# A recurrent network's kernel: TensorE's two nested loops become one flat loop whose jump lies between two matmul groups, and GpSimd's sums lose their start gates

## What is computed

```python
Xz = jnp.einsum('btc,hc->tbh', X, Wxz) + bxz          # and Xr, Xh alike
def step(H, xs):
    Z = jax.nn.sigmoid(xz + H @ Whz.T + bhz)
    R = jax.nn.sigmoid(xr + H @ Whr.T + bhr)
    H_tilda = jnp.tanh(xh + R * H @ Whh.T + bhh)
    H_new = Z * H + (1.0 - Z) * H_tilda
    Y = H_new @ Whq.T + bhq
    return (H_new, Y)
_, Ys = jax.lax.scan(step, h0, (Xz, Xr, Xh))
x = x + jnp.transpose(Ys, (1, 0, 2))
```

## Time and profile before

| | |
|---|---|
| median of 3 runs | 2247.37 us (2243.91 to 2275.53) |
| the profiled execution | 2232.23 us, its span 2230.3 us |
| PE busy | 2132.6 us, 96% |
| DVE, ACT, POOL busy | 71%, 55%, 40% |
| TensorE clock granted | 0.998 of full speed (2.4 GHz) |

### The profile page before, as it was taken

How to read it: one execution, slowest core, us unless ns; L and a number is a source line. 1 busy time by engine, 2 the same in 40 slices (tenths; PEclk the granted TensorE clock), 3 DMA queues, 4 the chain that set the end, 5 groups by cost and what they waited for, 6 DMA issues and landing times.

```text
span 2230.3 us, 206497 instructions
## 1 busy us (share of the span) xinstructions
PE 2132.6 (96%) x88464; PEld 2054.4 (92%) x88464; DVE 1589.5 (71%) x9106; ACT 1226.0 (55%) x5994; POOL 888.9 (40%) x1830
## 2 busy tenths in 40 slices
PE   8899999999999999999999999999999999999997
PEld 7799999999999999999999999999999999999997
DVE  4777777777777777777777777777777777777776
ACT  2455555555555555555555555555555555555554
POOL 3344344444344443444443444434444434444331
PEclk9999999999999999999999999999999999999999
DMA  3000000000000100000000000000000000000000
GB/s 153 16 28 17 26 24 21 26 24 21 26 24 19 28 17 26 24 21 26 24 21 26 23 19 28 16 26 24 21 26 24 21 26 24 19 28 16 26 20 22
DMA packets 84278, 58.27 MB, mean 26 GB/s; under 512 B 9490, under 2 KB 75410, under 8 KB 83474
## 3 DMA queue, kind: packets, MB, share of 16 engines
q1 hardware_dynamic: 84240, 57.81, 8.7%
q10 hardware_dynamic: 4, 0.02, 0.0%
HBM read 41.01 MB, written 16.78 MB: 26 GB/s over the span
## 4 chain that ended last, share of the span: by engine, by line
PE 95%; issue 4%; DMA 1%; DVE 1%; ACT 0%; SPq 0%; DVEq 0%
PE u_bank L620 42%; PE v_bank L620 20%; PE y_bank L555 9%; PE d_bank L523 7%; PE b_bank L523 6%; PE a_bank L523 6%; PE c_bank L523 3%; DMA w_all<-in_w_x 0%; PE b_bank L540 0%; PE a_bank L540 0%; PE u_bank L540 0%; DVE pre_t L980 0%; PE c_bank L540 0%; DMA y_io<-in_x_res 0%; DVE scanned L1082 0%
## 5 line engine op out<-in xcount | busy, mean ns | idle before, releaser
L980 DVE STREAM_TRANSPOSE pre_t<-u_bank 128x32 f32<-128x32 f32 (+1 forms) x3072 | 455.1, 199 | 278.2 <-PE u_bank L620 241.4
L620 PE MATMUL u_bank<-wh,scanned 128*16 128x128 f32 (+1 forms) x16384 | 548.5, 273 | 82.8 <-issue 74.9
L317 POOL TENSOR_TENSOR x_parts<-z_of 128x96 f32<-128x96 f32 x744 | 341.6, 459 | 556.7 <-DVE h_sums L1000 243.1
L620 PE MATMUL u_bank<-wh,reset_state 128*16 128x128 f32 (+1 forms) x16384 | 556.4, 273 | 3.7 <-DVE reset_state L1133 2.5
L620 PE MATMUL v_bank<-wh,scanned 128*16 128x128 f32 (+1 forms) x16384 | 548.1, 273 | 0.0
L620 PEld LDWEIGHTS u_bank<-wh,scanned 128*16 128x16 f32 (+1 forms) x16384 | 428.5, 103 | 112.4 <-issue 103.7
L620 PEld LDWEIGHTS v_bank<-wh,scanned 128*16 128x16 f32 (+1 forms) x16384 | 460.9, 104 | 0.3 <-issue 0.2
L620 PEld LDWEIGHTS u_bank<-wh,reset_state 128*16 128x16 f32 (+1 forms) x16384 | 428.4, 103 | 18.2 <-DVE reset_state L1133 14.0
L968 ACT ACTIVATE scan_on<-pre_t 128x16 f32<-128x16 f32 (+1 forms) x1536 | 237.8, 219 | 288.8 <-DVE pre_t L980 288.8
L942 ACT ACTIVATE r_gate<-pre_t 128x16 f32<-128x16 f32 (+1 forms) x1536 | 234.5, 215 | 255.4 <-DVE pre_t L980 247.9
L317 POOL TENSOR_TENSOR z_of<-z_of 128x96 f32<-128x96 f32 x558 | 255.9, 459 | 275.5 <-DVE reset_state L1133 173.1
(11 more groups left out here) (141 smaller groups left out, 2848.9 us busy)
## 6 DMA issues: line engine op xcount, KB each, us to landing
y_io<-in_x_res SPq DMA_DIRECT2D x256, 64.0 KB, 2.0
out<-y_io SPq DMA_DIRECT2D x256, 64.0 KB, 1.6
x_all<-in_x_t SPq DMA_DIRECT2D x62, 256.0 KB, 2.6
w_all<-in_w_x SPq DMA_DIRECT2D x2, 1536.0 KB, 7.6
wh<-in_w_hr SPq DMA_DIRECT2D x1, 1024.0 KB, 10.7
wh<-in_w_hz SPq DMA_DIRECT2D x1, 1024.0 KB, 14.2
wh<-in_w_hh SPq DMA_DIRECT2D x1, 1024.0 KB, 16.2
wq<-in_w_q SPq DMA_DIRECT2D x1, 1024.0 KB, 6.4
```

The lines of the kernel that those rows point to most:

```text
L317: nc.gpsimd.tensor_tensor(*of, ALU.add).then_inc(made, 1)
L620: mm = nc.tensor.matmul(gate_rows(g, par, slice(Q * j, Q * j + rows)), of, wh[g][:, m, P * j:P * (j + 1)], start=False, stop=(m == G - 1), ...
L980: nc.vector.transpose(flat(pre_t[g][:, a:b]), gate_part(g, par, a, b)).then_inc(done, 1)
```

## The change

On PE, `half_turn` becomes `steps`, which starts with Z of its first step and ends with R of the next half's first step; one flat loop ("four_steps") over four steps takes the place of the two nested ones, so the jump back stands between R and Z. The loop's counters are registers, added to between matmul groups, and the hint for the jump's target is given once, in the body's first step. Which of the two products lists runs is chosen by a register, `begins`. The last three halves are written out behind the loop. The waits for `u_put` and `v_put` move: `u_put` to a place ahead of gap work in the step before, `v_put` in front of R's last four matmuls. Waits for `x_loaded` and `s_ready` move from PE to ACT, ahead of the copies that PE waits for anyhow, and waits for weight sums move to the block that needs them. On POOL, all four gates go, and with them the increments of `kept_ready` on DVE.

```diff
                 elif before:
-                    after_sums(2 * n)
                     combine_x2(6, n - 2)
                     combine_x2(7, n - 2)
-                    after_reset(t)
                     combine_21(3, n - 2)
-                    after_kept(t)
                     combine_21(4, n - 2)
-                    after_state(t + 1)
                     combine_21(5, n - 2)
...
-            def half_turn(i, t, x_gap, first=False, end=False):
...
+            def steps(at, x_gap, within=None, end=False, first=False):
...
                 for c in range(4):
-                    par, s = divmod(c, 2)
...
-                    recur(R, t + c, c)
+                    if c > 0:
+                        recur(R, t + c + 1, c, i if c == 2 and not first else None)
+                        if within is not None and c > 1:
+                            within(c)
                     if first and c == 0:
                         plain_to(2, a_bank)
...
-                    recur(Z, t + c, c)
+                    recur(Z, None, c, first=first and c == 0)
...
+                    if c == 3 and not end:
+                        pe.wait_ge(u_put[0], i + 1)
                     x_gap(c)
...
+                if not end:
+                    recur(R, t + 5, 0, i + 1)
...
-            with nc.Fori(0, turns - 1, engines=[mybir.EngineType.PE], head_slot={mybir.EngineType.PE: 0}, hint_back_edge=True) as n:
-                with nc.Fori(0, 2, engines=[mybir.EngineType.PE], hint_back_edge=True) as later:
-                    half_turn(2 * n + 1 + later, 8 * n + 4 + 4 * later, lambda c: batch_gap(c, n, later))
...
+            with nc.body("four_steps", valid_engines=[PE]):
...
+                    if c == 1:
+                        batch_now.append(pe.snap(batch, min_val=1, max_val=turns))
+                        here.append(pe.mark_branch_hint_location())
+                    elif c == 2:
+                        pe.reg_add(halves, halves, 1)
+                    elif c == 3:
+                        pe.reg_add(steps_done, steps_done, 4)
...
+                        if c == 3:
+                            pe.reg_mov(begins, 0)
...
+                back = pe.br_lt(steps_done, 8 * turns - 12, on_true="four_steps", on_false="last_steps")
+                back.branch_hint(here[0])
...
             def a_to_b(k):
                 act.wait_ge(p1a_done, k + 1)
+                act.wait_ge(s_ready[2], k + 1)
```

More of the change, by code:

```diff
@@ L602, in project_y, with recur @@
                 return mm
-            def recur(g, t, c):
+            def recur(g, ready, c, put=None, first=False):
                 par, s = divmod(c, 2)
-                if isinstance(t, int) and t == 0:
+                if first:
                     pe.wait_ge(wh_loaded[g], 16)
@@ L610, in recur @@
                         if m == a and g == R:
-                            pe.wait_ge(state_ready[h], t + 1)
+                            pe.wait_ge(state_ready[h], ready)
                         if m == a and g == H:
-                            pe.wait_ge(reset_ready[h], t + 1)
+                            pe.wait_ge(reset_ready[h], ready)
+                    if m == G - 1 and put is not None:
+                        pe.wait_ge(v_put[par], put)
                     if g == H:
@@ new lines, in _, with now, within, batch_gap @@
+            steps(lambda: (0, 0), plain_gap, first=True)
+            steps_done, halves, batch, begins = (pe.alloc_register(n) for n in ("steps_done", "halves", "batch", "begins"))
+            for register, value in ((steps_done, 4), (halves, 1), (batch, 1), (begins, 1)):
+                pe.reg_mov(register, value)
+            pe.addr_align(256, offset=0, max_nops=0)
+            pe.br("four_steps")
+            with nc.body("four_steps", valid_engines=[PE]):
+                def now():
+                    return (pe.snap(halves, min_val=1, max_val=2 * turns),
+                            pe.snap(steps_done, min_val=4, max_val=8 * turns))
+                def within(c):
+                    if c == 1:
+                        batch_now.append(pe.snap(batch, min_val=1, max_val=turns))
+                        here.append(pe.mark_branch_hint_location())
+                    elif c == 2:
+                        pe.reg_add(halves, halves, 1)
+                    elif c == 3:
+                        pe.reg_add(steps_done, steps_done, 4)
+                def batch_gap(c):
+                    k = batch_now[0]
+                    with pe.If_ne(begins, 0):
+                        if c == 0:
+                            with pe.If_ne(batch, 1):
+                                batch_ends(k - 1)
+                        batch_begins(c, k)
+                        if c == 3:
+                            pe.reg_mov(begins, 0)
+                    with pe.Else():
+                        batch_goes_on(c, k)
+                        if c == 3:
+                            pe.reg_mov(begins, 1)
+                            pe.reg_add(batch, batch, 1)
+                here, batch_now = [], []
+                steps(now, batch_gap, within)
+                back = pe.br_lt(steps_done, 8 * turns - 12, on_true="four_steps", on_false="last_steps")
+                back.branch_hint(here[0])
@@ L773, in _ @@
+            nc.switch_bb("last_steps")
+            steps(lambda: (2 * turns - 3, 8 * turns - 12), last_gap)
+            steps(lambda: (2 * turns - 2, 8 * turns - 8), lambda c: None)
+            steps(lambda: (2 * turns - 1, 8 * turns - 4), lambda c: None, end=True)
             project_y(1).then_inc(y_projected, 1)
```

192 lines of the change are left out of this document (81 added, 111 removed).

## The result

The changed kernel is slower: 2267.89 us, median of four executions (2267.15 to 2268.08), against 2245.64 us before (2230.99 to 2275.53). The ratio is 1.012, with a 95% interval of 1.0072 to 1.0169: slower, clear of the interval, but by less than 2%. The forecast was 2194 us, its range 2145 to 2255. Executions of one kernel, above all of the kernel before, can take some per cent longer at a lower granted clock, so each ratio here compares only those within 1.5% of the fastest of their kernel. The profiled execution took 2267.15 us, its span 2265.4.

A forecast was written before the change was run, and what follows sets the result against it. PE bounds the kernel; gaps removed, jump residue and DVE holds added give 33.18 us a turn instead of 34.07: -55 us over about 62 turns, 2 added for the first turn, 2179 us, plus 15 for the median: 2194, range 2145 to 2255.

The forecast's parts named there:

- What bounds the kernel: PE, busy 96% of 2230.3 us; without its 1.84 us of gaps a turn of eight steps would take 32.23 us.
- The jump: PE's loop jumps: covered by queued matmuls, removing gaps of 1.12 (outer) and 0.44 us (inner) a turn; cost taken as 0.
- residue: PE between gap work and R: setting `begins`, a jump over the other list, one register addition; 0.13 us a turn.
- The gates: Without them POOL's sums hold up DVE's scans, `reset_state` and `kept`: 2.3 us a turn, of which 0.82 reach PE.
- short run: POOL's ten sums starting when the new x is there, in step 1: 4.9 us, with 0.08 between sums.
- long run: POOL's nineteen sums starting after PE's `batch_ends`, in step 4's gap work: 11.4 us, through steps 5 and 6 into 7.
- My walk: POOL's sums laid end to end against DVE's wants per step, each held until 0.14 us before a running sum's end.
- the lock becomes the bound: Rival, chance 0.13: POOL sums slip between two DVE scans, holding each group twice; 2.6 us a turn at PE, 2302 us.
- point of no change: DVE holds reaching PE at 1.7 us a turn would leave the kernel's time unchanged; 2.4 would make it 2% slower.
- The cover: PE's slack over the chain through the other engines (3.89 us a step against 4.03): 0.14 us a step on average.
- the jump isn't covered: Rival, chance 0.05: PE's jump still costs 0.44 us twice a turn; a turn of 34.06 us, 2247 us.
- fetches its target anew: Rival, chance 0.02: each of PE's 124 jumps back costs 2.2 us more for instruction fetch; 2465 us.

The follow-up runs named there:

- the two undisturbed kernels: Changed kernel with POOL's sums replaced by one-column sums and non-reading fills, 2113.29 us; changed kernel with gates back and sums dealt out anew, 2111.69 us.
- the one execution of 3646 us: Slowest of four executions of the changed kernel with POOL's sums replaced by one-column sums and non-reading fills; 3646.11 us, median 2113.29 us.

## Why the prediction was wrong

**What bounds the kernel: right.** PE's own 32.23 us a turn without gaps, worked out from start to start, is what the two undisturbed kernels reach (32.18).

**The jump: right, and a little too careful.** Forecast: -1.12, -0.44, -0.20, -0.08 and a residue of +0.13, together 32.36 us. The steps show -1.14, -0.41, -0.23 and -0.10, and no residue that can be told: 32.18.

**The gates: the mechanism right, its size wrong, and this decided the sign.** Scans are locked out as `reset_state` is, in two dense runs a turn. The term that failed is the +0.82 us a turn that meetings were to bring to PE; it measured 2.44. The holds and what reached PE, in us a turn, the latter against the undisturbed 32.18:

| | holds forecast | holds measured | at PE forecast | at PE measured |
|---|---|---|---|---|
| short run, steps 1 and 2 | 0.82 | 0.81 | 0.50 | 0.54 |
| long run, steps 4 to 7 | 1.52 | 2.76 | 0.32 | 1.90 |

For the short run each number holds. Its sums, all but one, do wait for one another and lie 0.08 us apart, as the forecast had it. For the long run two steps of the working failed.

- *The gap between sums.* I took 0.08 us from two sums of the earlier trace rows, where the second waits for the first. Sums that don't wait for their forerunner start 0.04 us before it ends, and ten of the long run's seventeen successions are of that kind. The trace before had such pairs too (1032.16 + 0.67 = 1032.83, next at 1032.79):

```profile
1032.16 0.67 POOL L306 TENSOR_TENSOR x_sub<-x_all,x_sub 128x224 f32<-128x224 f32 x1 [0.86 <-DVE scanned L1082]
1032.79 0.66 POOL L308 TENSOR_TENSOR x_sub<-x_all 128x224 f32<-128x224 f32 x1
```

With 0.14 us of letting in, what is open is about 0.10 us and not 0.22, so only one DVE instruction passes. My walk held a group up once and then let it go through. The trace has three scans held in step 5 for 1.14 us where I had 0.21, two `reset_state` parts there for 0.85 where I had 0.07, and one scan in step 4, where the run begins, for 0.46 where I had none. Behind that it has less than I had: 0.2 us in steps 6 and 7 instead of 0.91, for without the gaps the run lasts 9.9 us and not 11.4 and is over before step 7. It was the rival "the lock becomes the bound", in which a sum slips in between two scans, that told the mechanism right. I gave it 0.13, because a run meets only some ten groups. The trace has even fewer, nine in a turn, but within a group the instructions are held one after another. Of its figures, 2.48 us reached PE and it said 2.6, a turn of 34.96 and 2302 us, where 34.66 and 2268 were measured. That they lie so near is in part luck, as its 2.6 was not worked out from rows. The time is past its point of no change (1.7 us a turn) and short of its 2% (2.4, with the residue that I had on the jump).

- *The cover.* Of 1.52 us in the long run I let 0.32 reach PE. Of the measured 2.76, 1.90 did. The rows of PE above show why for the scans of step 5: R wants them one after another and is idle twice, for 0.20 and 0.49 us, so a cover of 0.14 us a step, which I had named, is soon used up. What each hold alone passed on to PE was not measured.

The sum with the measured terms: 32.18 + 0.54 + 1.90, and 0.04 in step 0, is 34.66, as measured.

**Against its own time, or the median.** I added 15 us, since the shown median before was that much above its profile. The changed kernel's four executions lie within 0.9 us, its median 0.7 above its profile; against its own profile the forecast of 2179 us misses by 88, and the 15 made the miss look smaller. The spread belonged to the nested loops, not to the work: all flat kernels with the hint repeat within 5 us but for the one execution of 3646 us, while executions of the kernel before range from 2227 to 2396 us in these comparisons. The fetches seen in the trace of the nested loops without gates would fit, but no trace of one of these longer executions is kept, and the cause of the spread is open.

**The other rivals.** That the jump isn't covered, and that it fetches its target anew, are both out for the changed kernel (222 ns, 28 packets). The second exists after all: in the old nested loops, when POOL's gates are taken away.

## What to carry to other kernels

A wait that isn't for data may be the very thing that keeps two engines' instructions apart; before it goes, count the instructions of the bounded chain that can meet what it holds back, one by one and not by groups, and take the spacing of the other engine's instructions from rows in which none waits for its forerunner. A dense run on a helper engine is worse than a spread one even when it is shorter, and the cheap repair was to deal its work out into the stretches in which the chain isn't on DVE. When an edit has two parts, price and run each alone: here one alone was worth -97 us against the median before and the other +120, and the two together looked like a failed idea.

## What the runs showed of the hardware that I had not expected

- POOL's sums overlap by 0.04 us in their recorded times where the second doesn't wait for the first, and still one DVE instruction passes at each end (step 5: three scans held in turn, for 0.49, 0.43 and 0.22 us).
- A POOL instruction that only writes leaves DVE's two-input instructions alone (343 at 179 ns), and such work between sums, which opens 0.14 us more between two sums, made the whole kernel 62 us faster, though POOL does more.
- Two nested loops whose jumps have hints can fetch their body again in a third of the rounds (21 of 64 jumps, up to 5.2 us each, 201 packets on the instruction queue instead of 21), in an otherwise regular program, while no profile of a flat loop here shows a long jump back. With the gaps the granted clock falls to 1.2 GHz for 3.4 to 10.2 us a turn, and together they cost some 13 us a turn.
